# The edge passes of two graph attention layers with the programs of SyncE, VectorE and TensorE written out chunk by chunk

## The chip, the cores and the metric

One core of one Trainium2 chip. The metric is the device time of one execution in microseconds (us); the time given is the median of several runs.

## The reference

The program computes a layer norm and a two-layer GraphSAGE network, and then two layers of graph attention (a transformer convolution) on 200,000 edges sorted by their target node. The change touches the edge part of the attention layers alone, which is in the reference:

```python
def _transformer_conv(h, src, tgt, edge_attr, Wq, bq, Wk, bk, Wv, bv, We, Wskip, bskip, Wbeta):
    q = (h @ Wq + bq).reshape(n, HEADS, C)
    k = (h @ Wk + bk).reshape(n, HEADS, C)
    v = (h @ Wv + bv).reshape(n, HEADS, C)
    e = (edge_attr @ We).reshape(-1, HEADS, C)
    k_j = k[src] + e
    alpha = jnp.einsum('ehc,ehc->eh', q[tgt], k_j) / jnp.sqrt(jnp.float32(C))
    amax = jax.ops.segment_max(alpha, tgt, num_segments=n)
    ex = jnp.exp(alpha - amax[tgt])
    denom = jax.ops.segment_sum(ex, tgt, num_segments=n)
    a = ex / denom[tgt]
    msg = (v[src] + e) * a[..., None]
    out = jax.ops.segment_sum(msg, tgt, num_segments=n).reshape(n, HID)
```

There are 4 heads of 32 channels. The gate with `Wbeta` and the batch norm that follow are computed elsewhere (`conv_after`).

## The kernel before

`program` calls `conv_edges` once for each of the two attention layers (tags conv0 and conv1), each followed by `conv_after`. The edges lie in 1664 steps of 128 edges, all edges of a step having their targets in one block of 128 nodes. A chunk is 32 steps (`CH`), so a pass has 52 chunks, or 26 pairs (`PAIRS`). A chunk is handled in 8 groups (`KG`) of 4 steps (`GR`), and its sums in 16 pairs of steps (`KP`).

Five engines work on a pass, each with its own program, in step by semaphores that count up through the whole pass:

- SyncE loads the chunk's tables: source numbers, edge terms, block numbers, penalties, steps, target places. It starts on them when `scored` (L1429) says that the scores of an earlier chunk are made, and waits on `wd_used` (L1432), `blk_used` (L1436), `rel_used` and `place_used` as their buffers come free. Each pair of chunks has 26 transfers.
- GpSimd gathers a key and value row for each edge, one indirect DMA a step (L1457), 32 a chunk. There are two chunks' worth of buffers (`kv`), so a group's gathers wait until TensorE's sums have read the older rows (`sums_ready`, L1453).
- ScalarE makes selection matrices from target numbers (`select`, `select_turned`, L1735 to L1764) and the exponentials of the softmax (L1778, L1780).
- TensorE picks the queries of each edge by a matrix product (`queries`, L1664), transposes the scores (L1688), spreads maxima over steps (L1693 to L1706), and makes each step's weighted sums (`sums`, L1678) in three PSUM banks.
- VectorE multiplies queries with keys (L1478) and reduces them to scores (L1483), adds the edge terms (L1533, then L1535, whose end raises `scored`), runs the softmax of the chunk over its 32 steps (L1538 to L1579; L1547 waits for TensorE's `ends_summed`), weights the values (L1506), and adds the step's sums into the table of its block of nodes (L1606). Which block is read from memory: `blocks_of` loads 16 numbers into registers (`load`), and they make the addresses.

The work of two chunks is interleaved: `stages(a, b)` of an engine scores chunk a (groups 3 to 7 beside the sums of b) while it finishes chunk b. A chunk is a triple (c, h, g): its number, its half of the buffers and its pair. In a loop c and g come from the loop's register, and so do wait values such as `KP * c + j + 1`. VectorE, TensorE and ScalarE have the first stage or two and the last ones written out, and a hardware loop (`Fori`) over pairs between. In VectorE's case the loop is made by `Chain.turns` (L91), with its `Fori` at L95, which also gives the waits of VectorE on its own semaphore (`need`, `mark`) a base that grows with each turn. A turn of VectorE's loop begins with L1533 of an odd chunk, and an even chunk's L1533 is in the middle of it.

Of the kernel before, what the change touches and what calls it, by code (L numbers as in the profile page):

```python
# [41 lines left out]
KG = CH // GR  # L42
# [3 lines left out]
PAIRS = NC_ // 2  # L46
# [1288 lines left out]
def chunk(g, half):  # L1335

    return g * 2 + half, half, g
# [3 lines left out]
KP = CH // PAIR  # L1341
# [8 lines left out]
def conv_edges(nc, t, tag):  # L1350

    with room(nc, tag) as (sb, psum, sem):
# [63 lines left out]
        with nc.Block() as block:  # L1416
            @block.sync
            def _(sp):
                flat = t.place_d.rearrange("c n -> (c n)")
                steps = t.b_d.rearrange("c n -> (c n)")  # L1420

                def places(c, h, g, q):
                    sp.wait_ge(place_used, 4 * c + q + 1)
                    sp.dma_start(place[:, q % 2, :], flat[bass.ds(c * (CH * P) + q * (2 * GR * P), 2 * GR * P)]
                                 .partition_broadcast(P)).then_inc(place_in[q % 2], 16)

                with sp.Fori(0, PAIRS) as g:
                    for h in range(2):
                        c = g * 2 + h  # L1429
                        sp.wait_ge(scored, c + 1)  # L1430
                        sp.dma_start(src[:, h, :], t.src_d[:, bass.ds(c * CH, CH)]).then_inc(src_in[h], 16)
                        sp.wait_ge(wd_used, c + 1)  # L1432
                        sp.dma_start(wd[:, h, :, :], t.edge_d[:, 1:3, bass.ds(c * CH, CH)]).then_inc(wd_in[h], 16)
                        places(c, h, g, 0)
                        places(c, h, g, 1)
                        sp.wait_ge(blk_used, c + 1)  # L1436
                        sp.dma_start(blk[:, h, :], steps[bass.ds(c * CH, CH)].rearrange("(a n) -> a n", a=1)).then_inc(blk_in[h], 16)
                        for k in range(HEADS):
                            sp.dma_start(pen[CH * k:CH * k + CH, h, :], t.pen_d[bass.ds(c * CH, CH), :]).then_inc(wd_in[h], 16)
                        sp.dma_start(stp[:, h, :, :], t.step_d[bass.ds(c * CH, CH), :].partition_broadcast(HEADS)).then_inc(wd_in[h], 16)  # L1440
                        places(c, h, g, 2)
                        sp.wait_ge(rel_used, c + 1)
                        sp.dma_start(rel[:, h, :], t.edge_d[:, 0, bass.ds(c * CH, CH)]).then_inc(rel_in[h], 16)
                        places(c, h, g, 3)
# [17 lines left out]
            def _(dve):  # L1462
                chain = Chain(dve, chain_v)
# [170 lines left out]
                for k in range(KG):  # L1634
                    scores(chunk(0, 0), k)
                stages(chunk(0, 1), chunk(0, 0))
                with chain.turns(PAIRS - 1, 2 * (2 * KG + 15 + KP)) as g:
                    stages(chunk(g + 1, 0), chunk(g, 1))
                    stages(chunk(g + 1, 1), chunk(g + 1, 0))
                stages(None, chunk(PAIRS - 1, 1))  # L1640
# [2 lines left out]
            def _(pe):  # L1643
# [76 lines left out]
                    queries(chunk(0, 0), k, at)  # L1720
                queries(chunk(0, 1), 0, blocks_of(chunk(0, 1), 0))
                stages(chunk(0, 1), chunk(0, 0), chunk(1, 0))
                with pe.Fori(0, PAIRS - 2) as g:
                    stages(chunk(g + 1, 0), chunk(g, 1), chunk(g + 1, 1))
                    stages(chunk(g + 1, 1), chunk(g + 1, 0), chunk(g + 2, 0))
                stages(chunk(PAIRS - 1, 0), chunk(PAIRS - 2, 1), chunk(PAIRS - 1, 1))
# [456 lines left out]
```

## Time and profile before

| | before |
| --- | --- |
| median of 3 runs | 12163.2 us |
| lowest and highest | 12148.79 and 12170.95 us |
| the profiled execution | 12124.6 us, span 12122.7 us |
| TensorE busy, instructions | 5591.6 us (46%), 23720 |
| VectorE | 3794.2 us (31%), 11057 |
| ScalarE | 4685.4 us (39%), 11029 |
| GpSimd | 6650.8 us (55%), 6852 |

The rows come from one profiled execution of that program. Times are in us from the start of the span, unless marked ns. PE is TensorE, DVE VectorE, ACT ScalarE, POOL GpSimd and SP SyncE; a q behind it is the engine's sequencer, the part that reads its instructions, waits and branches. A row of a timeline has the start, the busy time, the engine, the line of the kernel, the operation, its operands (out<-in) and, in brackets, how long the engine was idle ahead of it and what ended that; "issue" means that it waited for nothing that the profile shows, "remote" that it waited for a semaphore whose sender couldn't be told.

### The profile page before, as it was taken

Reading aid. Unit: us, or ns where it says so; the run is one execution under the profiler, and the core shown is the slowest. Engines: PE = TensorE matmul, PEld = TensorE weight load, DVE = VectorE, ACT = ScalarE, POOL = GpSimd, SP = SyncE. Lnnn points to the kernel's source line nnn. Section 1 sums busy time; section 2 is a strip of 40 time slices with the busy share of each in tenths; the row PEclk is TensorE's granted clock in tenths of the full one; section 3 lists DMA queues with packets and bytes.
Section 4 is the critical chain, followed back from the end, with each engine's and each line's share of the span. In section 5 each row is a group of like instructions: output and inputs, shape, how many; then the busy total and the mean of one; then the engine's idle time right before and its main releaser. Section 6 shows DMA issues by size and latency. Waiting matters only on the chain. (4 is left out here: it accounts for less than half of the span.)

```text
span 12122.7 us, 136052 instructions
## 1 busy us (share of the span) xinstructions
PE 5591.6 (46%) x23720; PEld 4740.3 (39%) x23721; DVE 3794.2 (31%) x11057; ACT 4685.4 (39%) x11029; POOL 6650.8 (55%) x6852
## 2 busy tenths in 40 slices
PE   0333333344443343454555555555645555555556
PEld 0333333333333333333444444444434444444444
DVE  3000000001000000034445554544744455545447
ACT  2333333333333333343444444444334444444443
POOL 4665555554565555555555555555445555555555
PEclk8555555566555555566666666666866666666667
DMA  5111111124111111134333333333243333333333
GB/s 102 50 52 49 49 50 49 49 65 128 49 51 50 48 48 49 48 104 124 113 112 112 111 113 110 111 114 113 79 131 112 111 112 109 115 111 111 113 113 88
DMA packets 623121, 1069.90 MB, mean 88 GB/s; under 512 B 213469, under 2 KB 396798, under 8 KB 622482
## 3 DMA queue, kind: packets, MB, share of 16 engines
q0 software_dynamic: 261920, 645.88, 19.2%
q1 hardware_dynamic: 281842, 368.09, 9.7%
q10 hardware_dynamic: 78848, 51.39, 1.5%
q14 instruction: 468, 3.83, 0.1%
q8 instruction: 43, 0.70, 0.0%
HBM read 961.58 MB, written 103.26 MB: 88 GB/s over the span
## 5 line engine op out<-in xcount | busy, mean ns | idle before, releaser
L1457 POOL DMA_INDIRECT conv_kv<-key_value,conv_src x3328 | 3287.0, 988 | 2925.8 <-PE conv_ps_sums L1678 1423.8
L1678 PE MATMUL conv_ps_sums<-conv_kv,conv_sel 128*128 128x136 f32 x6656 | 1509.3, 388 | 1428.2 <-DVE sums L1606 1124.7
L765 POOL DMA_INDIRECT second_msg<-sage_hidden_projected,second_src x1564 | 1477.1, 944 | 1135.3 <-SPq L727 534.2
L765 POOL DMA_INDIRECT first_msg<-sage_in,first_src x1564 | 1477.1, 944 | 1058.4 <-SPq L727 516.6
L1678 PEld LDWEIGHTS conv_ps_sums<-conv_kv,conv_sel 128*128 128x128 f32 x6656 | 1315.2, 280 | 1573.7 <-DVE sums L1606 1212.6
L1758 ACT ACTIVATE conv_selT<-conv_place,minus_partition 128x512 f32<-128x512 f32 x832 | 595.5, 716 | 3094.5 <-PE conv_ps_query L1664 1087.7
L1664 PE MATMUL conv_ps_query<-query_table,conv_selT 128*128 x6656 | 1585.8, 413 | 325.4 <-issue 277.2
L1664 PEld LDWEIGHTS conv_ps_query<-query_table,conv_selT 128*128 128x128 f32 x6656 | 1410.6, 308 | 420.6 <-issue 406.4
L870 PE MATMUL first_ps_sums<-first_msg,first_sel 128*128 x3328 | 832.0, 429 | 1524.4 <-ACTq L788 786.1
L870 PE MATMUL second_ps_sums<-second_msg,second_sel 128*128 x3328 | 832.7, 429 | 1473.6 <-ACTq L788 789.6
L1606 DVE TENSOR_TENSOR sums<-sums,conv_ps_sums 128x136 f32 x3328 | 972.5, 292 | 1506.2 <-remote 732.8
L870 PEld LDWEIGHTS first_ps_sums<-first_msg,first_sel 128*128 128x128 f32 x3328 | 718.5, 319 | 1651.1 <-issue 1651.1
L870 PEld LDWEIGHTS second_ps_sums<-second_msg,second_sel 128*128 128x128 f32 x3328 | 719.7, 319 | 1586.0 <-issue 1586.0
L1743 ACT ACTIVATE conv_sel<-iota_row,conv_rel 128x128 f32<-128x128 f32 x3328 | 1051.9, 386 | 59.7 <-PE conv_ps_sums L1678 59.1
L795 ACT ACTIVATE second_sel<-iota_row,second_rel 128x128 f32<-128x128 f32 x1664 | 556.9, 392 | 1185.0 <-issue 961.8
L795 ACT ACTIVATE first_sel<-iota_row,first_rel 128x128 f32<-128x128 f32 x1664 | 557.4, 392 | 1162.4 <-issue 922.6
L1478 DVE TENSOR_TENSOR conv_kv<-conv_ps_query,conv_kv 128x512 f32<-128x512 f32 x832 | 572.2, 688 | 1073.4 <-DMA after_hT<-conv_in_transposed 355.4
L834 DVE COPY sums<-second_ps_sums 128x129 f32 (+1 forms) x98 | 28.7, 293 | 2447.3 <-PE second_ps_sums L870 1112.0
L834 DVE COPY sums<-first_ps_sums 128x129 f32 (+1 forms) x98 | 28.7, 293 | 2426.5 <-PE first_ps_sums L870 1113.0
L1483 DVE TENSOR_REDUCE conv_score<-conv_kv 128x16 f32<-128x512 f32 x832 | 568.0, 683 | 0.0
L1763 ACT ACTIVATE conv_selT<-conv_selT 128x512 f32<-128x512 f32 x832 | 523.9, 630 | 61.9
L1746 ACT ACTIVATE conv_sel<-conv_sel 128x512 f32<-128x512 f32 x832 | 523.9, 630 | 26.3
(255 smaller groups left out, 5229.3 us busy)
## 6 DMA issues: line engine op xcount, KB each, us to landing
conv_place<-place_rows SPq DMA_DIRECT2D x416, 512.0 KB
conv_kv<-key_value,conv_src POOLq DMA_INDIRECT x3328
first_msg<-sage_in,first_src POOLq DMA_INDIRECT x1564
second_msg<-sage_hidden_projected,second_src POOLq DMA_INDIRECT x1564
conv_pen<-run_penalties SPq DMA_DIRECT2D x416, 48.5 KB
sage_own_hidden<-first_own_out ACTq DMA_DIRECT2D x49, 256.0 KB
sage_dense_own<-sage_own_hidden SPq DMA_DIRECT2D x14, 896.0 KB
sage_hidden_transposed<-sage_dense_hid SPq DMA_DIRECT2D x14, 896.0 KB
```

Source lines behind the costliest of these rows:

```text
L765: pool.indirect_dma_start(msg[:, j * MW:j * MW + D], None, table, bass.IndirectOffsetOnAxis(ap=src[:, b, j:j + 1], axis=0)).then_inc(gathe ...
L795: act.activation(sel[:, lo + i, :], t.iota[:, :], ACT.Abs, bias=rel[:, bass.ds(c * CH + (k * GR + i), 1)], scale=-1.0).then_inc(away_ready, 1)
L870: last = pe.matmul(ps[:, bass.ds(to[j] * 512, MW)], sel[:, h * CH + k * GR + i, :], msg[:, bass.ds(at[j] * MW, MW)], start=False, stop=Fal ...
L1457: pool.indirect_dma_start(kv[:, h * CH + j, :], None, t.kv_d, bass.IndirectOffsetOnAxis(ap=src[:, h, j:j + 1], axis=0)).then_inc(gathered[ ...
L1478: return mark(dve.tensor_tensor(keys, query(k)[:, :, :, 0:D], keys, ALU.mult))
L1483: return mark(dve.tensor_reduce(score[:, h, :, k * GR:k * GR + GR].rearrange("p h i -> p i h"), slots(h, k)[:, :, 0:D].rearrange("p i (h c ...
L1606: ins = dve.tensor_tensor(acc, acc, sums_of(h, step), ALU.add)
L1664: last = pe.matmul(psQ[:, 2 * (k % 2) + i // 2, (i % 2) * QW:(i % 2) * QW + QW], selT[:, k % SELG, P * i:P * i + P], t.qreg[:, bass.ds(at[ ...
L1678: last = pe.matmul(sums_of(h, step), sel[:, k % SELG, step % GR, :], kv[:, h * CH + step, DEN:2 * D], start=True, stop=True)
L1743: act.activation(sel[:, k % SELG, i, :], t.iota[:, :], ACT.Abs, bias=rel[:, h, j:j + 1], scale=-1.0).then_inc(away_ready, 1)
L1746: act.activation(sel[:, k % SELG, :, :], sel[:, k % SELG, :, :], ACT.Relu, bias=1.0, scale=-1.0).then_inc(sel_ready, 1)
L1758: act.activation(selT[:, k % SELG, :], place[:, q % 2, (k % 2) * GR * P:(k % 2 + 1) * GR * P], ACT.Abs, bias=t.minus[:, 0:1]).then_inc(awa ...
```

## The change

Three loops over pairs of chunks become loops of the program that writes the kernel, so that each pair has its own instructions, with constants where the loop's register was: SyncE's, VectorE's and TensorE's. VectorE's waits on its own semaphore then count on through the whole pass. The loops of GpSimd (26 turns) and ScalarE (24 turns) stay. No operation of the computation, no buffer and no order changes.

```diff
@@ -1424,7 +1424,7 @@
                     sp.dma_start(place[:, q % 2, :], flat[bass.ds(c * (CH * P) + q * (2 * GR * P), 2 * GR * P)]
                                  .partition_broadcast(P)).then_inc(place_in[q % 2], 16)
 
-                with sp.Fori(0, PAIRS) as g:
+                for g in range(PAIRS):
                     for h in range(2):
                         c = g * 2 + h
                         sp.wait_ge(scored, c + 1)
@@ -1634,7 +1634,7 @@
                 for k in range(KG):
                     scores(chunk(0, 0), k)
                 stages(chunk(0, 1), chunk(0, 0))
-                with chain.turns(PAIRS - 1, 2 * (2 * KG + 15 + KP)) as g:
+                for g in range(PAIRS - 1):
                     stages(chunk(g + 1, 0), chunk(g, 1))
                     stages(chunk(g + 1, 1), chunk(g + 1, 0))
                 stages(None, chunk(PAIRS - 1, 1))
@@ -1720,7 +1720,7 @@
                     queries(chunk(0, 0), k, at)
                 queries(chunk(0, 1), 0, blocks_of(chunk(0, 1), 0))
                 stages(chunk(0, 1), chunk(0, 0), chunk(1, 0))
-                with pe.Fori(0, PAIRS - 2) as g:
+                for g in range(PAIRS - 2):
                     stages(chunk(g + 1, 0), chunk(g, 1), chunk(g + 1, 1))
                     stages(chunk(g + 1, 1), chunk(g + 1, 0), chunk(g + 2, 0))
                 stages(chunk(PAIRS - 1, 0), chunk(PAIRS - 2, 1), chunk(PAIRS - 1, 1))
```

## Rows read from the trace of the kernel before

**Rows 1.** The page, costliest groups: busy us, mean ns, idle before and its releaser.

```profile
L1457 POOL DMA_INDIRECT conv_kv<-key_value,conv_src x3328 | 3287.0, 988 | 2925.8 <-PE conv_ps_sums L1678 1423.8
```

**Rows 2.** Timeline of VectorE, lines L1535 and L1533 alone, both passes.

```profile
5601.29 0.29 DVE L1535 TENSOR_TENSOR conv_score<-conv_score,conv_wd 128x128 f32<-128x128 f32 x1
...
5658.15 0.29 DVE L1535 TENSOR_TENSOR conv_score<-conv_score,conv_wd 128x128 f32<-128x128 f32 x1
...
5714.66 0.29 DVE L1535 TENSOR_TENSOR conv_score<-conv_score,conv_wd 128x128 f32<-128x128 f32 x1
...
6954.40 0.29 DVE L1535 TENSOR_TENSOR conv_score<-conv_score,conv_wd 128x128 f32<-128x128 f32 x1
...
7010.00 0.29 DVE L1535 TENSOR_TENSOR conv_score<-conv_score,conv_wd 128x128 f32<-128x128 f32 x1
...
7071.45 0.35 DVE L1533 TENSOR_TENSOR conv_score<-conv_score,conv_qwe 128x128 f32<-128x128 f32 x1 [3.54 <-issue]
7071.83 0.29 DVE L1535 TENSOR_TENSOR conv_score<-conv_score,conv_wd 128x128 f32<-128x128 f32 x1
...
8485.51 0.29 DVE L1535 TENSOR_TENSOR conv_score<-conv_score,conv_wd 128x128 f32<-128x128 f32 x1
...
8541.28 0.29 DVE L1535 TENSOR_TENSOR conv_score<-conv_score,conv_wd 128x128 f32<-128x128 f32 x1
...
8985.40 0.29 DVE L1535 TENSOR_TENSOR conv_score<-conv_score,conv_wd 128x128 f32<-128x128 f32 x1
...
9043.99 0.29 DVE L1535 TENSOR_TENSOR conv_score<-conv_score,conv_wd 128x128 f32<-128x128 f32 x1
...
9106.41 0.29 DVE L1533 TENSOR_TENSOR conv_score<-conv_score,conv_qwe 128x128 f32<-128x128 f32 x1 [3.06 <-issue]
```

**Rows 3.** Idle time ahead of L1533 (104 times issued): us, times.

```profile
  issue: 153.0, 48
```

**Rows 4.** L95 in 6950 to 6955: count, duration ns, first and last start.

```profile
L95 DVEq COMPARE_BRANCH  x1: 68/68/68, 6950.4 to 6950.4; - x1
L95 DVEq FUSED_REGOPS  x1: 85/85/85, 6953.8 to 6953.8; - x1
```

**Rows 5.** Timeline of GpSimd, single gathers of both passes.

```profile
5618.22 2.51 POOL L1457 DMA_INDIRECT conv_kv<-key_value,conv_src  x1 [32.04 <-PE conv_ps_sums L1678]
...
5674.68 2.17 POOL L1457 DMA_INDIRECT conv_kv<-key_value,conv_src  x1 [9.47 <-PE conv_ps_sums L1678]
...
6969.87 2.38 POOL L1457 DMA_INDIRECT conv_kv<-key_value,conv_src  x1 [12.16 <-PE conv_ps_sums L1678]
...
7015.95 0.95 POOL L1457 DMA_INDIRECT conv_kv<-key_value,conv_src  x1 [0.30 <-issue]
7027.98 2.46 POOL L1457 DMA_INDIRECT conv_kv<-key_value,conv_src  x1 [11.09 <-PE conv_ps_sums L1678]
...
9003.29 2.17 POOL L1457 DMA_INDIRECT conv_kv<-key_value,conv_src  x1 [11.41 <-PE conv_ps_sums L1678]
...
9063.68 2.20 POOL L1457 DMA_INDIRECT conv_kv<-key_value,conv_src  x1 [13.57 <-PE conv_ps_sums L1678]
```

**Rows 6.** Timeline of VectorE, line L1547, three chunks of the first pass.

```profile
5664.01 0.27 DVE L1547 TENSOR_TENSOR_SCAN conv_fromleft<-conv_stp,conv_fromleft,conv_ps_small 4x32 f32<-4x32 f32 x1 [1.47 <-remote]
...
7017.84 0.27 DVE L1547 TENSOR_TENSOR_SCAN conv_fromleft<-conv_stp,conv_fromleft,conv_ps_small 4x32 f32<-4x32 f32 x1 [3.48 <-remote]
...
8547.33 0.27 DVE L1547 TENSOR_TENSOR_SCAN conv_fromleft<-conv_stp,conv_fromleft,conv_ps_small 4x32 f32<-4x32 f32 x1 [1.74 <-remote]
```

**Rows 7.** Timeline of VectorE, adds of L1606 in the loop and written out.

```profile
7031.02 2.47 DVE L1606 TENSOR_TENSOR sums<-sums,conv_ps_sums 128x136 f32 x6
...
7036.82 1.60 DVE L1606 TENSOR_TENSOR sums<-sums,conv_ps_sums 128x136 f32 x4
...
8595.94 0.73 DVE L1606 TENSOR_TENSOR sums<-sums,conv_ps_sums 128x136 f32 x2 [0.22 <-DVE sums L1606]
```

**Rows 8.** What SyncE waited for: us in total, times, longest us.

```profile
SPq L1437 <- DVEq L1514: 2176.8, 100, 22.4
```

## The prediction, made before the result was known

> **What bounds the kernel now.** I read the page first for its span and its costliest groups [rows 1], then the starts of one line of VectorE that is issued once a chunk, which gives the period, then what ended the idle time before that line, and last GpSimd's gathers, since they set when a chunk can begin. The line is L1535, the last operation before `scored` rises; call its start T(c). One pass has 52 chunks. From T(0) to T(50) the first pass takes (8541.28 - 5601.29)/50 = 58.80 us a chunk [rows 2]; I take the second, which runs the same code, at the same. These 100 steps are about half of the span. They alternate. Into an even chunk, after the first half of VectorE's loop body, a step is short: 7010.00 - 6954.40 = 55.60 and 8541.28 - 8485.51 = 55.77. Into an odd chunk it is long: 7071.83 - 7010.00 = 61.83 [rows 2]. The long steps are those at whose end the engine comes back to the top of its loop. L1533, the first operation there, shows idle time put down to "issue", 153.0 us over 48 times, 3.19 each [rows 3]. Inside it the loop's compare-and-branch starts at 6950.4 and the next instruction of the engine only at 6953.8 [rows 4]. That is 3.4 us in which the engine waits for no semaphore.
>
> No engine is full. GpSimd's gathers wait most for TensorE's sums [rows 1], TensorE waits for VectorE, and so round: the chunk is a ring of dependences, and what counts is when each of its links is released.
>
> **A sum for one step.** I split a step at A(c), the start of the first of the long run of gathers that follows T(c) by 15 to 20 us. It can't start before the first sums of TensorE, so it marks the end of the softmax of the chunk. From A(c) to the next T, without the stall at L1533, it is nearly constant: 5714.66 - 5674.68 = 39.98, 7010.00 - 6969.87 = 40.13, 7068.29 - 7027.98 = 40.31 (3.54 of stall taken off 7071.83), 9043.99 - 9003.29 = 40.70, and 9103.67 - 9063.68 = 39.99 (9106.41 is L1533's start; L1535 follows by about 0.32, and 3.06 of stall is off) [rows 2, 5]. What varies is the part up to A. After a stall: 6969.87 - 6954.40 = 15.47. After a T without a stall: 5674.68 - 5658.15 = 16.53, 7027.98 - 7010.00 = 17.98, 9003.29 - 8985.40 = 17.89, 9063.68 - 9043.99 = 19.69 [rows 2, 5]. The reason lies in the last eight gathers of the chunk before, which go on across T. At 7010 their last one ends at 7015.95 + 0.95 = 7016.90, and VectorE's L1547, which waits 3.48 for a signal of TensorE, starts at 7017.84 [rows 5, 6], 0.94 behind it. While gathers are issued, TensorE's signals come late. A stall of VectorE lets these gathers run out meanwhile, and the chunk behind it is shorter by some 2.5 us (17.98 against 15.47). So most of the stall's price is given back today, and taking the stall away takes that gift away too.
>
> **The change, part by part.**
> VectorE (L1637). The 48 returns to the top go: 48 x 3.19 = 153 us [rows 3], all on the path, because L1533 is the next link. At once every T is a T without a stall. The four samples above have 18.02 to A in the mean and 40.25 behind it (39.98, 40.31, 40.70, 39.99), together 58.27. But only in two of them, 16.53 and 17.89, was T reached in written-out code on VectorE and TensorE, which is what the change makes of all; they give 17.21 + 40.25 = 57.46. In the first of them L1547 starts 5664.01 - 5658.15 = 5.86 us behind T and in chunk 50, reached with TensorE's code written out, 8547.33 - 8541.28 = 6.05, against 7.84 at 7017.84 [rows 2, 6]. I take the middle, 57.87. Of the 100 steps the first of each pass is written out already; 98 change: (58.80 - 57.87) x 98 = 91 us saved. Bounds: 16.53 and 39.98 make 56.51 a step and save 224 us; 19.69 and 39.99 make 59.68 and lose 86.
> The waits of VectorE become constants. The one place where constant waits show is the written-out stages. There two adds of L1606 take 0.73 + 0.22 = 0.95 us (chunk 51); in the loop, six take 2.47 and four 1.60, so two take 0.87 [rows 7]. The written-out form is slower by 0.08 us for two. With 16 such pairs a chunk that is 1.3 us at most, 125 us in all; at least nothing. I take nothing: the step 5601.29 to 5658.15 was run with written-out adds on VectorE and takes 56.86, of it 5658.15 - 5618.22 = 39.93 behind A, no longer than the loop's 40.25 [rows 2, 5]. The adds mostly wait for TensorE, and this hides it; if the cover is gone, up to 1.3 us a chunk comes back. Block numbers are still read from memory into registers, so the loads and address sums stay.
> TensorE (L1723). Its return lies at a place where it next waits for `scored`, that is for VectorE. The step 8485.51 to 8541.28 had TensorE on written-out code and VectorE in its loop: 55.77 against 55.60 [rows 2]. Zero, from -0.2 to +0.2 us a step; 20 us either way.
> SyncE (L1427). It waits 2176.8 us for VectorE to free the block numbers, 100 times [rows 8]. It issues the same 26 transfers in a pair of chunks, in the same order, behind the same waits; only their addresses no longer come from registers. Its program is early by no more than its own address sums, and the transfers are bounded by what frees their buffers. Zero; what covers it is that wait of 21.8 us a time.
> GpSimd and ScalarE keep their loops, so their waits against register values stay and nothing moves past them.
> The sum is -91, made against the profiled execution's 12124.6 us (its span is 12122.7), which gives 12034. The median of the runs is 12163.2, 38.6 above it; by that 12072.
>
> Against this stands the page "Advanced Engine Details and Errata" of the Trainium skill, section Control Flow Timing, which gives a compare-and-branch about 108 ns. By it 48 returns would be worth an estimated 5 us and the change nothing that can be measured. The row of the trace has 3.4 us [rows 4], so here the measurement decides.
>
> **The rivals.**
> 1. No change, all given back. If the short steps are 55.7 in the mean, as the two shown, the long ones must be 2 x 58.80 - 55.7 = 61.9 for the mean step to come out, and without the stall of 3.19 that is 58.7. A chunk behind a T without a stall would then cost nearly what the mean step costs now: 0.1 x 98 = 10 us saved, 12153. For it: three of the four A are 17.9 or more. Against it: the early ones, 16.53 and 16.93 (5618.22 - 5601.29, in a chunk with no gathers ahead of it) [rows 2, 5]. Chance 0.17.
> 2. A larger gain. TensorE's signals pass before the gathers end, as at 5658.15, and all steps take 56.5: 224 us saved, 11939; with steps like the even ones, 55.7, it is 304 us and 11859. For it: 16.53 was measured with the gathers in the way, and L1547 comes 6 us behind T there and in chunk 50. Against it: 17.89 in the same place of the second pass. Chance 0.14.
> 3. Slower: the adds. If VectorE's 16 pairs of adds with constant waits become the link behind A (it decides from the point at which TensorE's sums are ready before VectorE asks), 16 x 0.08 = 1.3 us comes on each step: 125 us. With rival 1's 10 us saved it is 12278; with half of the adds on the path 12216. For it: TensorE's sums wait for L1606 in their turn. Against it: the 39.93 above. Chance 0.12.
> 4. Slower: reading the code. Straight code is fetched from memory only once, and if VectorE stops at every block of it as it does at the return, twice in a pair of chunks, that is 48 more stops of 3.19 than now, +153, 12316. Against it: between the returns the loop's body shows no such stop: all 48 are at L1533, one a turn [rows 3]. The page "Runtime: NRT & Kernel Launch", section Instruction fetch mechanics, of the Trainium skill says that the sequencer fetches ahead in straight code and that a taken branch out of its window is what stalls; by it this rival falls away and the 153 us go. Chance 0.05.
> That the change doesn't do what it says is true for two of its three lines, by the above; the third carries the sum.
>
> **How the numbers follow.** Forecast (30 to 153 us saved, 12010 to 12133) 0.52, rival 1 0.17, rival 2 0.14, rival 3 0.12, rival 4 0.05. The predicted time is 12072. The range takes in most of rival 2 and half of rival 3: 11900 to 12225. About 0.2%, 24 us, is what a measurement of this kernel can tell from no change. Faster by more: 0.52 + 0.14 = 0.66; within: 0.17; slower: 0.12 + 0.05 = 0.17.
>
> **What would show it.** At L1533 no idle time put down to issue; if it is still there, or is seen at other lines of VectorE 48 times or more, rival 4. Steps no longer alternate between 55.7 and 61.5 but lie near 57.9; the part behind A stays at 40.2 (if it is 41 or more, rival 3; the groups of L1606 then stand in twos at 0.95), and the part before A tells between forecast (17.6), rival 1 (18.5) and rival 2 (16.5). L1547 comes about 0.9 us behind the last gather. The prediction is wrong if VectorE's stall was hiding a wait of another engine that then takes its place, most likely one of TensorE or ScalarE for place rows, which would show as a longer wait at L1664 or L1758.

## The result and the profile after

| | before | after |
| --- | --- | --- |
| median (4 runs each) | 12164.4 us | 11795.9 us |
| lowest to highest | 12148.8 to 12171.0 | 11774.0 to 11816.3 |
| ratio | | 0.9699, 95% interval 0.9679 to 0.9718 |
| profiled execution | 12124.6, span 12122.7 | 11816.3, span 11814.5 |
| from T(0) to T(50), first and second pass | 2940.0, 2947.5 us | 2771.5, 2772.6 us |

The change makes the kernel 368 us faster, 3.0%. The forecast was 92 us faster, 12072, in a range down to 11900: the sign was right, the size wrong by a factor of four, and the time lies 104 us below the range. (The two profiled executions differ by 308 us: before's lies below its median, after's above.)

The stage before the first pass, whose code is unchanged, ends 42 us later in this profile (T(0) at 5642.81 against 5601.29). The gain is in the passes: 343 us in the two.

The timeline of VectorE of the kernel after, L1535 and L1547 alone, answers [rows 2] and [rows 6]:

```profile
5642.81 0.29 DVE L1535 TENSOR_TENSOR conv_score<-conv_score,conv_wd 128x128 f32<-128x128 f32 x1
...
6975.06 0.29 DVE L1535 TENSOR_TENSOR conv_score<-conv_score,conv_wd 128x128 f32<-128x128 f32 x1
...
7031.06 0.29 DVE L1535 TENSOR_TENSOR conv_score<-conv_score,conv_wd 128x128 f32<-128x128 f32 x1
...
7036.35 0.27 DVE L1547 TENSOR_TENSOR_SCAN conv_fromleft<-conv_stp,conv_fromleft,conv_ps_small 4x32 f32<-4x32 f32 x1 [0.99 <-remote]
...
7086.95 0.29 DVE L1535 TENSOR_TENSOR conv_score<-conv_score,conv_wd 128x128 f32<-128x128 f32 x1
...
8414.34 0.29 DVE L1535 TENSOR_TENSOR conv_score<-conv_score,conv_wd 128x128 f32<-128x128 f32 x1
```

Steps no longer alternate: 56.00 and 55.89 us here. And L1547 stands 5.29 us behind L1535, where it stood 7.84 behind at 7017.84. The gathers of that step, answering [rows 5]:

```profile
7028.48 0.94 POOL L1457 DMA_INDIRECT conv_kv<-key_value,conv_src  x1 [3.27 <-remote]
...
7047.23 2.49 POOL L1457 DMA_INDIRECT conv_kv<-key_value,conv_src  x1 [9.05 <-PE conv_ps_sums L1678]
```

A comes 16.17 us behind T and the next T 39.72 behind A. The two views together are the sum of the prediction with other values. Means over all steps 1 to 49 of both passes (T is the start of L1535, A the first gather of the long run behind it):

| | step | T to A | A to T | L1547 behind T |
| --- | --- | --- | --- | --- |
| before, from an even chunk | 62.16 | 18.87 | 43.29 | 8.45 |
| before, from an odd chunk | 55.79 | 15.99 | 39.80 | 5.51 |
| after, from an even chunk | 55.70 | 16.03 | 39.67 | 5.45 |
| after, from an odd chunk | 55.14 | 15.43 | 39.71 | 4.69 |

From the 48 even chunks with a stall at their end, 3.19 us of stall, 2.84 ahead of A and 0.43 behind it went; from the 50 odd ones 0.56 and 0.09. That is 153 + 136 + 21 + 28 + 4 = 342 us, the whole of it. The last column says where the part ahead of A shrank: L1547 comes 3.00 us earlier behind T in the even chunks and 0.82 in the odd ones. Between T and L1547 VectorE stood idle for 4.13 and 1.20 us a chunk before, and for 1.23 and 0.49 after.

What ended the idle time ahead of L1533 and of L1547 (us, times), first after, then L1547 before. The names of transfers and "remote" both stand for a semaphore's late arrival, since L1547 waits for TensorE's `ends_summed` alone:

```profile
  issue: 0.3, 2
```

```profile
  DMA key_value<-after_work: 27.9, 19
  remote: 23.7, 19
  issue: 16.7, 8
  PE conv_ps_small L1694: 8.4, 32
```

```profile
  DMA key_value<-after_work: 72.4, 38
  remote: 72.3, 36
  issue: 3.4, 3
  PE conv_ps_small L1694: 1.1, 3
```

The stalls are gone (153.0 in [rows 3]). The wait at L1547 fell from 149 us to 77. That is not all of it. In 17 of the 48 even chunks the kernel before waits for over 2 us at a product of L1478 between T and L1547, for other signals; these waits took 96 us in all before and nothing after. One such row of before, in the chunk whose T is 5949.53:

```profile
5958.01 0.69 DVE L1478 TENSOR_TENSOR conv_kv<-conv_ps_query,conv_kv 128x512 f32<-128x512 f32 x1 [5.28 <-remote]
```

TensorE itself is no earlier in nearly all chunks (in four even chunks of before it was 6 to 7 us late): here are its rows for L1694, the product whose end sends that signal, in before (T at 7010.00) and in after (T at 7031.06).

```profile
7013.01 0.29 PE L1694 MATMUL conv_ps_small<-step_of_row,conv_ends 128*4 128x32 f32 x2
```

```profile
7034.08 0.29 PE L1694 MATMUL conv_ps_small<-step_of_row,conv_ends 128*4 128x32 f32 x2
```

Both start 3.01 to 3.02 us behind T. What shrank is the time from TensorE's end to VectorE's start, from 4.54 us to 1.98. I call it the lateness of the signal; some 0.9 us of it is VectorE's own work (its L1483), for where it doesn't wait at all, in e14 below, the same figure is 0.90. The means below leave out the four chunks in which TensorE was late. VectorE's adds waited 732.8 us for signals whose sender isn't told before, and 106.6 after.

```profile
DVE sums L1606 <- remote: 732.8, 150, 7.8
```

```profile
DVE sums L1606 <- remote: 106.6, 64, 4.5
```

This is a shift more than a saving: all idle time ahead of L1606 fell from 1258 us to 608, but that ahead of L1478, which stands among the same adds, rose from 1071 to 1678.

### The profile page after: what moved, and what is told of

Same layout as the page of the kernel before. It is cut to its first block and busy times, and to the rows that moved or that the text cites. A ratio compares the mean times of both kernels' runs of the same rounds, so it can differ in the third digit from the quotient of the medians.

```text
span 11814.5 us, 123908 instructions
## 1 busy us (share of the span) xinstructions
PE 5381.6 (46%) x23720; PEld 4592.8 (39%) x23721; DVE 3788.8 (32%) x11057; ACT 4670.4 (40%) x11029; POOL 6634.3 (56%) x6852
## 5 line engine op out<-in xcount | busy, mean ns | idle before, releaser
L1678 PE MATMUL conv_ps_sums<-conv_kv,conv_sel 128*128 128x136 f32 x6656 | 1435.9, 381 | 1099.3 <-DVE sums L1606 1025.6
L1678 PEld LDWEIGHTS conv_ps_sums<-conv_kv,conv_sel 128*128 128x128 f32 x6656 | 1287.6, 277 | 1213.4 <-issue 603.9
L1664 PE MATMUL conv_ps_query<-query_table,conv_selT 128*128 x6656 | 1453.8, 387 | 293.5 <-issue 276.6
L1664 PEld LDWEIGHTS conv_ps_query<-query_table,conv_selT 128*128 128x128 f32 x6656 | 1289.5, 284 | 369.2 <-issue 346.1
L1606 DVE TENSOR_TENSOR sums<-sums,conv_ps_sums 128x136 f32 x3328 | 974.8, 293 | 773.1 <-issue 200.7
L1478 DVE TENSOR_TENSOR conv_kv<-conv_ps_query,conv_kv 128x512 f32<-128x512 f32 x832 | 569.3, 684 | 1678.5 <-remote 617.6
L1483 DVE TENSOR_REDUCE conv_score<-conv_kv 128x16 f32<-128x512 f32 x832 | 568.5, 683 | 0.1
L1688 PE MATMUL conv_ps_small<-identity,conv_score 128*128 128x128 f32 x104 | 46.3, 445 | 1074.1 <-DVE conv_score L1535 758.7
```

Of the source, the lines that this page charges most:

```text
L1478: return mark(dve.tensor_tensor(keys, query(k)[:, :, :, 0:D], keys, ALU.mult))
L1483: return mark(dve.tensor_reduce(score[:, h, :, k * GR:k * GR + GR].rearrange("p h i -> p i h"), slots(h, k)[:, :, 0:D].rearrange("p i (h c ...
L1606: ins = dve.tensor_tensor(acc, acc, sums_of(h, step), ALU.add)
L1664: last = pe.matmul(psQ[:, 2 * (k % 2) + i // 2, (i % 2) * QW:(i % 2) * QW + QW], selT[:, k % SELG, P * i:P * i + P], t.qreg[:, bass.ds(at[ ...
L1678: last = pe.matmul(sums_of(h, step), sel[:, k % SELG, step % GR, :], kv[:, h * CH + step, DEN:2 * D], start=True, stop=True)
```

## The experiments

The question was which line of the change carries the 343 us and whether a stall's price is given back. The runs landed on chips of two kinds, so each is compared with the kernel before on its own chip: 11954 to 11964 us on two chips that behave as the first profile does (e1 to e4 and e9 to e12 on one, e13 to e16 on the other), 9105 on two more (see e5).

**One line at a time, e1 to e3, and two together, e16.** Each edit is the line of the diff named, the others left as before:

```
e1:   -  with chain.turns(PAIRS - 1, ...) as g:    +  for g in range(PAIRS - 1):
e2:   -  with pe.Fori(0, PAIRS - 2) as g:          +  for g in range(PAIRS - 2):
e3:   -  with sp.Fori(0, PAIRS) as g:              +  for g in range(PAIRS):
e16:  e2 and e3
```

> VectorE's loop alone is written out (L1637); SyncE and TensorE keep theirs. Theory A (the gain is VectorE's 48 returns of 3.19 us and what hangs on them): nearly the whole of the change's 368 us, 11800 to 11850. Theory B (most of the gain is TensorE's: without register work its signals reach VectorE earlier while gathers are issued): about the 90 us of the prediction, 12030 to 12110, with L1547 still 7 to 8 us behind L1535. Theory C (SyncE's loads of place rows come earlier): as B here, 12030 to 12110.

> TensorE's loop alone is written out (L1723). Theory A: no change, 12165 within 25. Theory B: 200 us or more faster, under 11965, although VectorE's 48 stalls of 3.19 us at L1533 stay; L1547 comes 6 us or less behind L1535 in even chunks. Theory C: no change.

> SyncE's loop alone is written out (L1427). Theories A and B: no change, 12165 within 25. Theory C: 100 us or more faster; SyncE's wait at L1424 for ScalarE, 358 us in the kernel before and 838 in the changed one, is then near 838 here.

> SyncE's and TensorE's loops written out, VectorE's kept. If the two add, 63 + 65 = 128 us faster than before, 11830 (ratio 0.989), and VectorE's part is then 200 us of the 329: 158 for its returns and 42 for its constant waits. If both remove the same lateness, 65 us, 11895.

**VectorE's returns without its constants, e4:**

```
-                for g in range(PAIRS - 1):
-                    stages(...)
+                with chain.turns((PAIRS - 1) // 5, 10 * (2 * KG + 15 + KP)) as i:
+                    for r in range(5):
+                        g = i * 5 + r
+                        stages(...)
```

> The changed kernel, but VectorE's code is a hardware loop again, of 5 turns with 5 pairs of chunks written out in each: its waits go back to register values, its returns fall from 24 a pass to 4. This tells the returns from the constants. If the returns are what counts, the time is that of the changed kernel (11796) plus 8 x 3.2 = 26 us, 11800 to 11840. If the constant waits of VectorE carry a part, it is slower than that by their part, 11850 or more.

**The kernels themselves on those chips, e9 and e10:**

> The kernel before once more, for its profile beside the next three. Two kinds of chip have shown: one where it takes near 12000 us and GpSimd's gathers stop twice in a chunk for 3 us while TensorE's signals are late, and one where it takes 9109, its gathers run without a break at 1.25 us each and 32 of them, 40.0 us, are the step. If the kind is a property of the chip and of how fast signals pass, this profile is of one kind or the other as a whole: steps of 59 with breaks, or of 40.5 without.

> The changed kernel. On a chip with late signals: 230 us (theory A) to 370 us faster than before; the part ahead of A near 15.7 us. On one without: within 25 us of before, as GpSimd's 40.0 us a chunk bound both.

Measured, with the time of both passes in the profile, T(0) to T(50), the idle time ahead of L1547 in them and the mean lateness of its signal (even chunks, odd chunks):

| | us | against before | both passes | idle ahead of L1547 | lateness |
| --- | --- | --- | --- | --- | --- |
| e9, before | 11957 | | 5759 | 136 | 3.15, 2.08 |
| e2, TensorE | 11899.7 | 0.9955 (0.9937 to 0.9973) | 5720 | 136 | 2.66, 2.04 |
| e3, SyncE | 11901.7 | 0.9955 (0.9936 to 0.9975) | 5707 | 117 | 2.40, 2.02 |
| e16, SyncE and TensorE | 11874.6 | 0.9940 (0.9916 to 0.9963) | 5699 | 117 | 2.44, 1.91 |
| e1, VectorE | 11732.1 | 0.9815 (0.9795 to 0.9835) | 5525 | 96 | 2.29, 1.74 |
| e4, all three, VectorE in 5 turns | 11758.1 | 0.9837 (0.9812 to 0.9863) | 5573 | 126 | 2.38, 2.13 |
| e10, all three (after) | 11628.4 | 0.9721 (0.9698 to 0.9744) | 5433 | 34 | 1.52, 1.07 |

The ratio of e10 is near the first comparison's 0.9699, so this chip is fit for the question. No theory of one engine stands. VectorE alone brings 232 us of 329, of which its returns are 158 in e9 (157.9 us of issue at L1533); SyncE and TensorE alone bring 63 and 65, but together only 79, and once VectorE is written out 96 to 104. Of these small gains some 30 us aren't of the passes: the stages ahead of T(0), whose code is the same, end at 5544 to 5546 us in e2 and e3 and at 5576 in e9. In the passes SyncE alone brings 52 us, TensorE 39 and both 60. The theories that gave one of these two nothing (A) or all of the rest (B, C) each missed. e4 is the sharpest: against e10 only VectorE's form differs. It is 130 us slower. Its eight returns are in the trace:

```profile
  issue: 26.1, 8
```

They cost 26 us, so 104 us are left for VectorE's waits and addresses made from a register. It is 96 if each is taken against its own before (11964 and 11957, the same chip at two times) and 113 by the passes. That it is the register work, and not another difference between the two forms of the program, is the likely reading and not shown. e16 and e4 are the other half of the ladder: both keep VectorE's register work, and e4 has 8 returns instead of 48. So against before SyncE and TensorE bring 79 us, the 48 returns 127 + 26 = 153, and VectorE's constants 96. In e4 L1547 waits as in before,

```profile
  DMA key_value<-after_work: 64.3, 40
  remote: 50.3, 33
  issue: 10.7, 12
```

and in e10 hardly any more:

```profile
  remote: 11.7, 11
  DMA key_value<-after_work: 11.6, 11
  PE conv_ps_small L1694: 6.5, 31
  issue: 4.2, 5
```

**Is a stall given back? e8 and e12** put a stall of known length into the changed kernel, without a loop:

```
+                    if c % 2 == 1 and 3 <= c <= 49:
+                        for n in range(4):
+                            link(dve.memset(pad[:, :], 0.0))
                     m = mark(dve.tensor_tensor(near, near, qwe[:, :, :], ALU.add))
```

> The changed kernel with four chained memsets of 128x512 (about 3 us) ahead of L1533 in the odd chunks 3 to 49, the 24 places a pass where the loop's return was, without the loop. If most of a stall is given back in the next chunk (the prediction), it is slower than the changed kernel by under 50 us. If nothing is given back, by the full 48 x 3 = 144 us, and the part ahead of A behind those chunks stays at 15.5 to 16.

> As e8: about 3 us of memsets in the 24 places a pass where the loop's return was. With late signals: slower than the changed kernel by under 50 us if most of a stall is given back in the next chunk, by 144 if none is. With gathers that run without a break: under 25 us.

Timeline of VectorE in e12 (L1539 is L1535 of the other kernels, whose lines lie 4 lower):

```profile
7003.47 0.29 DVE L1539 TENSOR_TENSOR conv_score<-conv_score,conv_wd 128x128 f32<-128x128 f32 x1
...
7057.69 0.48 DVE L1536 MEMSET conv_pad<- 128x512 f32 x1 [0.30 <-issue]
7058.35 0.48 DVE L1536 MEMSET conv_pad<- 128x512 f32 x1 [0.17 <-DVE conv_pad L1536]
7059.01 0.48 DVE L1536 MEMSET conv_pad<- 128x512 f32 x1 [0.17 <-DVE conv_pad L1536]
7059.66 0.48 DVE L1536 MEMSET conv_pad<- 128x512 f32 x1 [0.17 <-DVE conv_pad L1536]
...
7060.51 0.29 DVE L1539 TENSOR_TENSOR conv_score<-conv_score,conv_wd 128x128 f32<-128x128 f32 x1
...
7115.02 0.29 DVE L1539 TENSOR_TENSOR conv_score<-conv_score,conv_wd 128x128 f32<-128x128 f32 x1
```

The next memset follows every 0.66 us, so four delay by 2.6, 48 times 126 us. e12 takes 11758.3 us against e10's 11628.4: 130 more. The step behind the stall is 54.51, and A behind those chunks comes 15.09 us after T in the mean, against 14.77 in e10. Nothing is given back: the passes are 145 us longer. In the changed kernel a stall is paid in full, and so the prediction's give-back is refuted, for this kind of chip. That holds with late signals and register work too. e4 still has eight stalls, and behind them the old gathers do run out earlier, 3.97 us behind T against 7.21, but A comes no earlier: 16.04 us behind T in the mean, against 15.93 in the other 42 odd chunks. One of the eight:

```profile
6156.01 0.29 DVE L1533 TENSOR_TENSOR conv_score<-conv_score,conv_qwe 128x128 f32<-128x128 f32 x1 [3.27 <-issue]
6156.33 0.29 DVE L1535 TENSOR_TENSOR conv_score<-conv_score,conv_wd 128x128 f32<-128x128 f32 x1
...
6172.50 2.18 POOL L1457 DMA_INDIRECT conv_kv<-key_value,conv_src  x1 [12.33 <-PE conv_ps_sums L1680]
```

And from e16 to e4 the idle time at L1533 falls by 134 us (160.5 to 26.1) and the passes by 126. (e8 ran on the other kind of chip, where the stall does come back: 9097.9 against 9088.6, 9 us of 126.)

**The phase, e7, e11, e13.** The last eight gathers of a chunk start 2.6 us ahead of T in the changed kernel and 2.9 to 3.2 in the even chunks of before's first profile, so lateness might hang on that. (In e9 they start 2.7 ahead in the mean, hardly another phase than e10's 2.6, with twice the lateness.) One line ahead of L1533, in after (e7, e11) and in before (e13):

```
+                    dve.memset(pad[:, 0:256], 0.0)
```

> The changed kernel with one memset of 128x256 ahead of L1533 in every chunk, so that L1535 comes later by the memset's time, about 0.3 us, against the last eight gathers (it starts 2.65 us behind the first of them in the changed kernel, 3.20 in even chunks of the kernel before). If lateness of TensorE's signal hangs on this phase, L1547 moves from 5 to 7 us or more behind L1535 and a step is longer by 1.5 us or more: 150 us and more slower than the changed kernel. If the phase plays no part, it costs its own 104 x 0.3 = 31 us.

> As e7: one memset of 128x256 ahead of L1533 in each chunk. With late signals, if their lateness hangs on the phase between L1535 and the last eight gathers (2.65 us in the changed kernel, 3.20 in even chunks of before): 150 us or more slower than the changed kernel, with L1547 at 7 us or more behind L1535. If not: 31 us, its own time. With gathers that run without a break: nothing, as in e7.

> The kernel before, all loops kept, with e11's memset of 128x256 (0.2 us) ahead of L1533 in each chunk. If the lateness of TensorE's signal is a matter of the phase between L1535 and the gathers alone, L1547 comes some 1 to 2 us nearer to TensorE's end in even chunks here too, and the kernel is 30 to 100 us faster than before in spite of 20 us of memsets. If it is the register work itself that makes it late, the kernel is 0 to 30 us slower.

e7, on the other kind of chip, 9091.9 against 9088.6: nothing, as expected of unbroken gathers. e11: 11591.6, 37 us faster than e10, although work was added. T came 0.2 us later against the gathers, and the idle time ahead of that kernel's L1547 (its L1549) is

```profile
  remote: 3.8, 3
  issue: 1.4, 2
  PE conv_ps_small L1696: 0.8, 2
```

with a lateness of 1.0 in all chunks. So the phase may count, and not in the direction I had named, but for less than 37 us: of the 51 us between the two profiled executions 29 lie ahead of T(0), the passes are 21 us shorter, and the intervals of e10 and e11 (0.9698 to 0.9744, 0.9683 to 0.9718) overlap. But in the kernel before it repairs nothing: e13 is 16 us slower (1.0015, 1.0003 to 1.0026), about its own 104 x 0.2 us, with a lateness of 3.33 and 1.64. Phase is not the cause of before's lateness; the expectation that it alone explains it falls.

**The other two engines, e14 and e15.** GpSimd's and ScalarE's loops written out too, e15 with e11's memset as well:

```
-                with pool.Fori(0, PAIRS) as g:          +  for g in range(PAIRS):
-                with act.Fori(0, PAIRS - 2) as g:       +  for g in range(PAIRS - 2):
```

> The changed kernel with GpSimd's and ScalarE's loops written out as well. Their returns cost 0.3 us and lie beside waits, so by the returns nothing: within 25 us of the changed kernel's 11628 (ratio 0.972). If each program without register work brings some 60 us through earlier signals, as SyncE's and TensorE's did, 11500 to 11570. On a chip whose gathers run without a break, nothing.

> e14 with e11's memset. If e14 gains nothing, this is as e11, 11590. If e14's signals are already at their earliest (1.0 us behind TensorE's end), the memset costs its own 20 us.

e14: 11580.3 us, 0.9687 (0.9661 to 0.9713) of before's 11953.9; e10 was 0.9721. The intervals overlap, and e14 ran on another chip of the same kind from e10's. In the trace the passes take 2693.3 and 2693.8 us against 2717.8 and 2715.6 in e10, and nothing is late at L1547 in any chunk:

```profile
7020.10 0.29 DVE L1535 TENSOR_TENSOR conv_score<-conv_score,conv_wd 128x128 f32<-128x128 f32 x1
...
7024.31 0.26 DVE L1547 TENSOR_TENSOR_SCAN conv_fromleft<-conv_stp,conv_fromleft,conv_ps_small 4x32 f32<-4x32 f32 x1
...
7073.94 0.29 DVE L1535 TENSOR_TENSOR conv_score<-conv_score,conv_wd 128x128 f32<-128x128 f32 x1
```

It stands 4.21 behind T, 0.90 behind TensorE's end, at the same phase as in e10, and VectorE isn't idle ahead of it. The memset of e15 then brings nothing (11562.8, ratio 0.9683, passes 2698.2 and 2697.3, a little longer, as its own time).

**Register work put back alone, e17 and e18.** e14 with 24 pairs of one engine in a loop of two turns, 12 pairs written out in each:

```
e17:  +  with chain.turns(2, 12 * 2 * (2 * KG + 15 + KP)) as z:  (pairs 1 to 24; pair 25 written out)
e18:  +  with pe.Fori(0, 2) as z:
```

> e14 (all five written out), but VectorE's pairs 1 to 24 are a hardware loop of two turns with 12 pairs written out in each: its waits and addresses are made in registers again, with one return a pass (6 us in all). If register work on VectorE makes signals late, L1547 goes back from 0.9 to 1.5 us or more behind TensorE's end and the kernel is 40 to 100 us slower than e14's 11580. If the returns alone counted, 5 to 10 us slower.

> e14, but TensorE's pairs are a loop of two turns of 12 pairs. If register work anywhere makes signals late, 30 to 70 us slower than e14, with L1547 later; if it counts on VectorE alone, nothing, within 15 us.

Both came to the kind of chip on which VectorE hardly waits at L1547 (0.8 us in all in e6): 9101.0 and 9086.9 us, before 9105.1. They don't answer their question. e17 is 14 us slower than e18, so VectorE's register work costs little there (its two returns are 6.4 us of the 14).

**The other kind of chip, e5 and e6.** Before and after, unchanged:

> The kernel before itself, unchanged, profiled on the chip of the next three, since its time moved by 200 us from chip to chip. If the 200 us lie in the part of a step ahead of the first gather A (18.9 us in the mean behind even chunks in the first profile), that part is near 16 here and its time near 11960; the stall at L1533 stays at 153 us. If they lie elsewhere, A stays at 18.9 and the part behind it or the other stages are shorter.

> The changed kernel, unchanged, on that chip. Where the kernel before takes 11960, theory A (VectorE's part is the whole) expects 11730 to 11760, a ratio of 0.981, as VectorE alone gave; if SyncE's and TensorE's parts (0.9955 each alone) add to it, 11600 to 11680.

Before takes 9108.9 us there and after 9088.6, a ratio of 0.9982 (0.9972 to 0.9991). GpSimd's timeline in e5:

```profile
5011.40 0.95 POOL L1457 DMA_INDIRECT conv_kv<-key_value,conv_src  x1 [0.30 <-issue]
5012.65 0.95 POOL L1457 DMA_INDIRECT conv_kv<-key_value,conv_src  x1 [0.30 <-issue]
5013.90 0.94 POOL L1457 DMA_INDIRECT conv_kv<-key_value,conv_src  x1 [0.30 <-issue]
```

It goes on so without a break, one in 1.25 us, and 32 are 40.0 us, the bound of a chunk. VectorE still stalls:

```profile
5004.60 0.29 DVE L1533 TENSOR_TENSOR conv_score<-conv_score,conv_qwe 128x128 f32<-128x128 f32 x1 [3.33 <-issue]
5004.92 0.29 DVE L1535 TENSOR_TENSOR conv_score<-conv_score,conv_wd 128x128 f32<-128x128 f32 x1
...
5042.86 0.29 DVE L1535 TENSOR_TENSOR conv_score<-conv_score,conv_wd 128x128 f32<-128x128 f32 x1
```

and the step behind the stall is 37.94, shorter than 40. The mean steps are 43.05 and 38.03 before, 40.24 and 40.35 after: here a stall is given back nearly whole, since gathers go on meanwhile. My guess for e5, that the part ahead of A would explain the chips' difference of 200 us, met a chip where the difference was 3000. On the chip of e9, 161 us lower in span than the first profile, the part ahead of A is 16.90 in even chunks against 18.87, 95 us of it.

## Why the prediction was wrong

- *What bounds the kernel; the stall at the returns.* Right. 153.0 us in the trace, 0.3 after, and nothing of the kind elsewhere: rival 4 fell, and the trace agrees with what the Trainium skill, "Runtime: NRT & Kernel Launch", Instruction fetch mechanics, says of straight code. Against the 108 ns of "Advanced Engine Details and Errata", Control Flow Timing, in the Trainium skill, the row was right to trust: e4's eight cost 26.1 us. The branch itself lasts 68 ns [rows 4]; the stop comes behind it, and in this loop of 443 instructions a turn. In a loop of 38 through the same L95, earlier in the same trace, the next instruction starts 0.19 us behind the branch.
- *"Most of the stall's price is given back."* This step failed first. Chunks behind a stall do have an earlier A in before (15.99 against 18.87), and I read it as a gift of the stall. No run bears that out: e12 pays 130 us for 126 of stall in the changed kernel, in e4 A is no earlier behind the stalls that are left, and e1, without any stall, still has its signals later in even chunks than in odd ones (2.29 and 1.74). Why before's even chunks are the late ones stays open. Nor does L1547 follow the last gather, as I had it from one chunk: in after it starts 5.45 us behind T in the even chunks, and the last gather ends 7.06 behind. Taking 57.87 for a step, I had paid for a loss that didn't come: the steps are 55.4 in the mean of the table, 2.4 us less. Of that, 1.9 is in the part ahead of A (17.6 in the sum, 15.7 measured) and 0.6 behind it (40.25, 39.69).
- *VectorE's constant waits: "I take nothing", up to 1.3 us a chunk slower.* Wrong in sign. Adds in twos at 0.94 us are there (L1606 waits for itself 673 times, 147.8 us in all, in the profile after), but beside waits. By e4 against e10 constants bring some 100 us (96 to 113). The samples I had, chunks 1 and 50, had only part of the programs written out; they showed L1547 at 5.86 and 6.05 instead of 7.84, and I took the middle between them and the loops where I should have asked what these rows have in common.
- *TensorE and SyncE: zero.* Wrong: 65 and 63 us alone (39 and 52 in the passes), 79 together, and by e1 against e10 92 to 104 once VectorE is written out. The argument, that they next wait for VectorE anyway, looked at when they start and not at how late their signals are.
- *Rival 2*, all steps like the short ones, 304 us saved, was the nearest to what came, at 0.14 and at the edge outside the range; the measured time is still 63 us below its 11859. Rivals 1 and 3 fell.
- *The range* left out the case in which both terms that I had set to nothing were gains.

What stays open is the mechanism. Shown is that lateness falls as programs are written out, which takes register work (waits against register values, addresses and counters) out of them: SyncE's, TensorE's and VectorE's each by itself, from 3.15 us in even chunks with all five in loops (e9) to 0.90 with none (e14, on another chip), and that it was seen only on the chips where gathers break. If phase has an influence, it is the smaller one. Not shown is whether the waits, the address sums or something else that a loop brings with it do it, nor why one kind of chip is free of it; e17 and e18, made for the first, met that kind.

## What to carry to other kernels

A wait for a signal has two parts, the sender's end and the signal's way; read both from the trace (the sender's row, then the waiter's) before calling an edit on an engine that "waits anyway" free. Where an engine stalls at the top of a long hardware loop, measure the idle time put down to issue there, and before crediting anything as given back, put a stall of known length in. And time such a change on more than one chip: the same edit gave 0.970, 0.972 and 0.998.

## What was not expected of the hardware

- The same kernel took 12164, 11957 and 9105 us on different chips. Most gathers took 0.95 us each on all. In the passes the difference is in breaks between them, one of 12 us and two of about 3 us a chunk in the first profile and none in e5; VectorE, idle for 149 us ahead of L1547 in the one, was idle there for 0.8 us in the other. The stages ahead of T(0) differ as well, 5601 us against 4472.
- A return to the top of VectorE's loop cost 3.2 us on both kinds (157.9 us for 48 in e9, 158.6 in e5).
- Work added ahead of `scored` (a memset, 0.2 us a chunk) didn't make the changed kernel slower: e11 is 37 us faster than e10 in the median and 21 in the passes, on the same chip, with intervals that overlap. The fastest kernel on a chip with late signals was e15 at 11562.8 us, 0.9683 of before, level with e14.
